# Second-order attention stage: units of one 128-token tile, or of two 64-token chunks from two batches

## Chip, core, metric

One Trainium2 chip, one of its cores. The metric is the device time of one execution in microseconds (us), lower is better. Before the change the kernel takes 3574.15 us, the median of three runs (3573.76 to 3574.67).

## What is computed

The reference is a chain of eight residual layers over x[8, 1024, 256] in float32. The change touches the fifth layer alone, a second-order linear attention with 16 heads of 32 columns and a decay of 0.99 per token:

```python
def step(carry, qkv):
    S_K, C_QV, G = carry
    q_t, k_t, v_t = qkv
    C_prev = GAMMA * C_QV
    k_C = jnp.einsum('bhk,bhkv->bhv', k_t, C_prev)
    G = GAMMA * G + k_t[..., :, None] * k_C[..., None, :]
    S_K = GAMMA * S_K + k_t[..., :, None] * k_t[..., None, :]
    C_QV = C_prev + q_t[..., :, None] * v_t[..., None, :]
    S_C = jnp.einsum('bhij,bhjv->bhiv', S_K, C_QV)
    o_t = jnp.einsum('bhk,bhkv->bhv', q_t, S_C - G)
    return ((S_K, C_QV, G), o_t)
...
x = x + _L1_attn_a_ref(_layernorm(x, axis=-1), L1_attn_a_Wq, L1_attn_a_Wk, L1_attn_a_Wv, L1_attn_a_Wo)
```

The other layers (local attention, two top-k expert layers, spectral attention, two tanh layers, window attention) are left as they are.

## The kernel before

The kernel runs its layers one after the other on one core; x stays in SBUF as 64 tiles of 128 tokens (`R.X`). `second_order_attention` (line 1544) is one stage. It does not walk token by token: it takes a tile of 128 tokens as a chunk, works out what the tokens of the chunk do to each other through masked 128x128 products, and carries a small state (three 32x32 matrices per head) from chunk to chunk.

**The unit.** One step `t` handles one tile for four heads (`HG = 4`, 4x32 = 128 partitions), so there are `NU` = 64 tiles x 4 head groups = 256 steps. Each engine has its own order of work, written out by hand as a loop over `t` (TensorE from line 1793, ScalarE 1908, VectorE 1988, GpSimd 2057), and semaphores tie them together. Within one step TensorE does, in this order:

- `keys_queries(t)` (L1647) and `queries_U(t-1)` (L1655): 8 and 4 matmuls on 32-row tiles of the array, 128 columns each, into the four banks `rows4`;
- `state_to_O(t-2)` (L1742, L1743): two matmuls over the whole array, against the state spread out to block-diagonal form by GpSimd (`spread_state`, L2045);
- `turn_KQ(t)`, `turn_W(t-1)` (L1668, L1669, L1662): three 128x128 transposes into `bankU`;
- a share of the projections of the tiles to come, in single-pass float32 (F32R), into `bankJ`: over 8 steps two of V (L1704), four of Q and K (L1684), the transposes of x (L1677), and two times the output projection `mix` (L1714), which goes to `bankX`;
- `state_to_UW(t)` (L1732, L1735): 8 matmuls on 32x32 tiles;
- `keys_to_U(t)`, `values_to_W(t)`, `values_to_O(t-1)` (L1749, L1756, L1763, L1766): 16 matmuls on 128x32 tiles; `state_products(t-1)` (L1777, L1780): 12 more with 32 columns.

ScalarE copies what comes out of PSUM (`copy_U` L1865, `copy_WT` L1869, `copy_O` L1878, `negate_W` L1892, `copy_KQ` L1898 and L1899, `copy_turned` L1852, `high_O` L1884); VectorE masks the 128x128 products (`mask_AB` L1965, `mask_P` L1973) and updates the state (`update` L1956); GpSimd applies the decay (L2032, L2039), spreads the state (L2045) and makes the low part of the output (`low_O` L2050).
## Time and profile before

| what | us |
|---|---|
| median of the runs | 3574.15 |
| profiled execution | 3566.9 |
| its span, first to last instruction | 3565.0 |
| this stage's loop, 1516 to 2750 us of the span | 1234 |
| TensorE busy in the loop | 1220.45 |
| ScalarE, VectorE, GpSimd busy in the loop | 577.49, 602.70, 518.98 |

The profile is of one execution. PE is TensorE's matmuls, PEld its weight loads, DVE VectorE, ACT ScalarE, POOL GpSimd. A matmul's end is modelled, so a PE that is busy all the time need not be full; the starts of instructions are the safer reading. PEclk is the share of TensorE's full clock that was granted. The queue named "instruction" carries the program itself to the engines.

### The profile page before, as it was taken

The numbers are of one execution on the slowest core, as the hardware profiler recorded it, in microseconds if no ns is written. First come the engines' busy times: TensorE is split into PE (matmuls) and PEld (weight loads), VectorE is DVE, ScalarE is ACT, GpSimd is POOL, SyncE is SP. The second block draws the span as 40 slices with busy tenths as digits, with TensorE's granted clock in tenths as the row PEclk, the third lists the DMA queues.
The fourth block names the chain that finished last, engine by engine and source line by source line (L and its number), as shares of the span: only waits on it lengthen the run. The fifth ranks groups of instructions, "written<-read, shape, count | busy, mean of one in ns | idle before, by whom it ended". The sixth has DMA issues, their size and how long they took to land. (4 is left out here: it accounts for less than half of the span.)

```text
span 3565.0 us, 133004 instructions
## 1 busy us (share of the span) xinstructions
PE 3316.4 (93%) x52918; PEld 2936.6 (82%) x52918; DVE 2212.0 (62%) x6377; ACT 2101.5 (59%) x6626; POOL 1505.2 (42%) x2318
## 2 busy tenths in 40 slices
PE   8939999799956999899999999999998999999998
PEld 8939999777746999888888888888887878888877
DVE  6675555678775555545544444444444788888887
ACT  5555655455445555444444444444443699999996
POOL 5754656300014665343434334344443633333225
PEclk9969999999977999999999999999999999999999
DMA  4143443512144443500000000000000143333333
GB/s 130 49 157 91 97 93 62 163 33 65 52 138 128 89 98 75 151 3 3 3 3 3 3 3 3 3 3 3 3 3 16 38 124 112 119 112 101 105 98 100
DMA packets 203003, 235.05 MB, mean 66 GB/s; under 512 B 18064, under 2 KB 183072, under 8 KB 202400
## 3 DMA queue, kind: packets, MB, share of 16 engines
q1 hardware_dynamic: 177824, 192.99, 17.1%
q0 software_dynamic: 24576, 33.57, 5.6%
q8 instruction: 433, 7.09, 0.8%
q14 instruction: 170, 1.39, 0.1%
HBM read 147.46 MB, written 79.04 MB: 64 GB/s over the span
## 5 line engine op out<-in xcount | busy, mean ns | idle before, releaser
L2513 ACT ACTIVATE wa_S<-wa_S,wa_top 128x192 f32<-128x192 f32 x1024 | 461.9, 472 | 38.7 <-DVE wa_top L2609 38.7
L1965 DVE TENSOR_TENSOR so_raw<-so_rows,so_masks 128x1024 f32<-128x1024 f32 x256 | 313.4, 1224 | 225.0 <-PE so_rows L1655 216.4
L2609 DVE CUSTOM_DVE_ANT_0 wa_S<-wa_bank,wa_band 128x192 f32<-128x192 f32 x1024 | 299.4, 348 | 3.6 <-issue 3.6
L2045 POOL TENSOR_TENSOR so_spread<-so_state,so_head 128x256 f32<-128x256 f32 x224 | 137.4, 613 | 336.5 <-PE so_bankC L1743 305.4
L1956 DVE SCALAR_TENSOR_TENSOR so_state<-so_state,so_bankX 128x96 f32<-128x96 f32 x192 | 48.8, 254 | 347.4 <-PE so_bankX L1780 347.4
L2050 POOL TENSOR_TENSOR so_OT<-so_O,so_OT 128x128 fp32r<-128x128 f32 x256 | 117.0, 457 | 343.3 <-ACT so_OT L1884 343.2
L1878 ACT COPY so_O<-so_bankC 128x128 f32<-128x128 f32 x256 | 68.1, 266 | 318.2 <-PE so_bankC L1743 318.1
L650 POOL DMA_INDIRECT sum_dram<-y,rows x128 | 223.8, 1749 | 29.5 <-issue 27.5
L2401 PE MATMUL wa_bank<-ident,wa_S 128*128 128x128 f32 x1536 | 220.9, 277 | 7.7 <-ACT wa_probT L2520 4.7
L2513 ACT ACTIVATION_READ_ACCUMULATOR wa_S<-wa_S,wa_top 128x1 f32 x1024 | 219.8, 215 | 0.0
L728 ACT ACTIVATE m4e_hT<-m_bank,m4e_bias 128x256 fp32r<-128x256 f32 x256 | 126.5, 494 | 150.1 <-PE m_bank L680 144.0
L728 ACT ACTIVATE m2e_hT<-m_bank,m2e_bias 128x256 fp32r<-128x256 f32 x256 | 125.9, 492 | 149.2 <-PE m_bank L680 142.8
L1684 PE MATMUL so_bankJ<-so_xnT,so_w 128*128 128x256 f32 x1500 | 207.8, 287 | 4.7 <-DVE so_xnT L1945 4.7
L2401 PEld LDWEIGHTS wa_bank<-ident,wa_S 128*128 128x128 f32 x1536 | 172.9, 140 | 36.1 <-ACT wa_S L2513 16.3
L680 PE MATMUL m_bank<-m4e_exT,m_w_parts 128*128 128x256 f32 x1536 | 189.9, 283 | 0.4 <-ACT m4e_h L728 0.4
L680 PE MATMUL m_bank<-m2e_exT,m_w_parts 128*128 128x256 f32 x1536 | 189.9, 283 | 0.0
L1684 PEld LDWEIGHTS so_bankJ<-so_xnT,so_w 128*128 128x128 f32 x1500 | 185.5, 190 | 5.1 <-DVE so_xnT L1945 5.1
L694 PE MATMUL m_bank<-m_w_parts,m4e_hT 128*128 128x256 f32 x1536 | 187.0, 281 | 0.6 <-DVE m4e_pre L775 0.6
L694 PE MATMUL m_bank<-m_w_parts,m2e_hT 128*128 128x256 f32 x1536 | 187.0, 281 | 0.6 <-DVE m2e_pre L775 0.6
L680 PEld LDWEIGHTS m_bank<-m4e_exT,m_w_parts 128*128 128x128 f32 x1536 | 184.2, 190 | 0.6 <-ACT m4e_h L728 0.6
L694 PEld LDWEIGHTS m_bank<-m_w_parts,m2e_hT 128*128 128x128 f32 x1536 | 184.0, 188 | 0.8 <-issue 0.8
L694 PEld LDWEIGHTS m_bank<-m_w_parts,m4e_hT 128*128 128x128 f32 x1536 | 184.0, 188 | 0.8 <-issue 0.8
(457 smaller groups left out, 9977.6 us busy)
## 6 DMA issues: line engine op xcount, KB each, us to landing
m_w_raw<-in_L_ffn_W_dram SPq DMA_DIRECT2D x64, 512.0 KB, 3.6
wa_V<-wa_V_dram SPq DMA_DIRECT2D x256, 128.0 KB, 2.6
sum_dram<-X SPq DMA_DIRECT2D x16, 1024.0 KB, 4.7
X<-sum_dram SPq DMA_DIRECT2D x16, 1024.0 KB, 8.2
wa_V_dram<-wa_V_new SPq DMA_DIRECT2D x32, 512.0 KB, 4.2
wa_V_rest<-wa_V_dram SPq DMA_DIRECT2D x128, 128.0 KB, 3.0
X<-in_L_attn_a_x_dram SPq DMA_DIRECT2D x8, 1024.0 KB, 10.9
xn_dram<-m2r_xn SPq DMA_DIRECT2D x16, 512.0 KB, 4.5
```

Source lines behind the costliest of these rows:

```text
L650: nc.gpsimd.indirect_dma_start(out=summed, out_offset=bass.IndirectOffsetOnAxis(ap=rows[:, s, u:u + 1], axis=0), in_=y[:, s % 2, u, :], in ...
L680: last = nc.tensor.matmul(bank[:, 0:2 * P], w_parts[:, par, a, c, f * P:(f + 1) * P], exT[:, s % 2, b, c], start=(n == 0), stop=(n == len( ...
L694: last = nc.tensor.matmul(by[u][:, 0:HID], hT[:, s % 2, a, f, u * P:(u + 1) * P], w_parts[:, par, b, 2 + f // QF, f % QF * HID:(f % QF + 1 ...
L728: last = nc.scalar.activation(to, bh[f % 4][:, 0:2 * P], ACT.Gelu_apprx_tanh, bias=bias[:, par, f:f + 1])
L1684: last = nc.tensor.matmul(bank[:, 2 * k * P:2 * (k + 1) * P], w[:, a, n, c, cols], xnT[:, b, c], start=(m == 0), stop=(m == 2 * len(PARTS) ...
L1878: nc.scalar.copy(O[:, t % UT], bC[:, P:2 * P]).then_inc(s_["O_copied"], 1)
L1965: nc.vector.tensor_tensor(AB[:, t % 2].rearrange("p h m t -> p h (m t)"), rows4[:, :, 0:2 * P], masks[:].rearrange("p m t -> p (m t)")[:, ...
L2045: nc.gpsimd.tensor_tensor(whole[:, t % UT], new[:, :, None, :].broadcast_to([P, 2, HG, DK]), head[:, None, :, None].broadcast_to([P, 2, HG ...
L2050: nc.gpsimd.tensor_tensor(OT[:, 1, t % (2 * UT)], O[:, t % UT], OT[:, 0, t % (2 * UT)].bitcast(F32), ALU.subtract).then_inc(s_["O_ready"], 1)
L2401: last = nc.tensor.transpose(to[:, h * P:(h + 1) * P], of, R.ident[:])
L2513: nc.scalar.activation(S[:, n % 2, z], S[:, n % 2, z], ACT.Exp, bias=top[:, n % 2, z:z + 1], scale=-1.0, accum_out=sums[:, i % 2, SET * c ...
L2609: nc.vector.tensor_tensor_reduce(out=S[:, n % 2, z], in0=bS[g][:, eo * SPAN:(eo + 1) * SPAN], in1=band[:], scale=-(D ** -0.5), scalar=3e38 ...
```

## The change

A unit becomes 64 tokens of two batches (`CHUNK` = 64, index `k`), still for four heads, so that the number of steps stays 256. Products that were 128x128 per head are now two of 64x64 (32x64 tiles), products over 128 tokens are two over 64 (64x32 tiles, one per batch, into two banks `cols`). The state's share of the output is computed on 32x32 tiles from the plain state, each head into the partitions of the next, and `spread_state` and its array go. `queries_U` and the outputs run a step later (`t-2`); VectorE copies the state's share out of `bankX` and adds it (`copy_from_state`, `add_O`) in place of ScalarE's `copy_O`; `copy_U` and `copy_WT` become one `copy_UW`; the three transposes share `bankX` and one semaphore; the output projection goes to `bankJ`, both tiles of a pair in the fourth step of eight, and the projections of Q and K to the last four. V and KW, KQe and AB get a third buffer. The order in which the 64 tiles of x are taken changes (pairs from two batches). GpSimd's `decayed`, `decayed_U`, `low_O` and `normalize` keep their sizes. The loads at the start: the output weights come in two DMAs, the masks at half size, `head` is gone.

The diff, cut; removed lines are left out where the kernel above has them:

```diff
+    CHUNK = P // 2
+    STEPS = SEQ // CHUNK
+        AB = raw[:, 0:3 * HG * P].rearrange("p (b h m t) -> p b h m t", b=3, h=HG, m=2)
+        PT = raw[:, 3 * HG * P:4 * HG * P].rearrange("p (b h t) -> p b h t", b=2, h=HG)
+        VRING = 3
+        V = sb("V", [P, VRING, UT, P])
+        KW, KQe = sb("KW", [P, 3, 2, P]), sb("KQe", [P, 3, 2, P])
+        UW, Ug = sb("UW", [P, 2, 2, P]), sb("Ug", [P, 2, P])
+        O, OT = sb("O", [P, UT, P]), sb("OT", [P, 2, UT, 2, 2, CHUNK], F32R)
+        from_state = sb("from_state", [P, 2, P])
+        rows4, cols = ps("rows", (P, HG, 512)), ps("cols", (P, 2, 512))
+        bX, bJ = (ps(f"bank{n}") for n in "XJ")
+        AT_U, AT_W, AT_O = (slice(n * CHUNK, (n + 1) * CHUNK) for n in range(3))
+        AT_S = slice(3 * CHUNK, 3 * CHUNK + 3 * DK)
...
+        def row_tile(p, half):
+            return (2 * (p // TB) + half) * TB + p % TB
+        def mixed_at(t):
+            return t // (2 * UT) - 1 if t % (2 * UT) == MIX_AT and t > MIX_AT else None
+                for to, name in ((masks[:, 0], "upper"), (masks[:, 1], "lower"), (decay_t[:], "decay_t"), (to_end[:], "to_end")):
+                out_rows = A["L1_attn_a_Wo"].rearrange("(u p) d -> p u d", p=P)
+                sp.dma_start(wo_raw[DK:P], out_rows[0:P - DK]).then_inc(s_["o_loaded"], 16)
+                sp.dma_start(wo_raw[0:DK], out_rows[P - DK:P]).then_inc(s_["o_loaded"], 16)
...
                 def keys_queries(t):
+                    ring, u, j = place(t)
+                    pe.wait_ge(s_["QT_ready"], halves_to(chunk(t)))
+                    pe.wait_ge(s_["KT_ready"], halves_to(chunk(t)))
                     for m, (a, b) in enumerate(((KT, QT), (QT, KT))):
                         for h in range(HG):
...
+                            for k in range(2):
+                                last = nc.tensor.matmul(rows4[half_rows(k), h, m * CHUNK:(m + 1) * CHUNK],
+                                                        a[head_rows(h), ring, u, j, half_rows(k)], b[head_rows(h), ring, u, j, half_rows(k)],
+                                                        start=True, stop=True, tile_position=(h * DK, k * CHUNK))
...
                 def queries_U(t):
+                    ring, u, j = place(t)
+                    pe.wait_ge(s_["UW_ready"], t + 1)
                     for h in range(HG):
...
+                        for k in range(2):
+                            last = nc.tensor.matmul(rows4[half_rows(k), h, 2 * CHUNK:3 * CHUNK],
+                                                    QT[head_rows(h), ring, u, j, half_rows(k)], UW[head_rows(h), t % 2, 0, half_rows(k)],
+                                                    start=True, stop=True, tile_position=(h * DK, k * CHUNK))
...
+                def turn(t):
+                    if t >= 3:
+                        pe.wait_ge(s_["from_state_ready"], carries_to(t - 3))
+                    if t < NU:
+                        at = place(t)
+                        nc.tensor.transpose(bX[:, P:2 * P], KT[(slice(None), *at)], R.ident[:])
+                        last = nc.tensor.transpose(bX[:, 2 * P:3 * P], QT[(slice(None), *at)], R.ident[:])
                     if t >= 1:
...
+                        pe.wait_ge(s_["UW_ready"], t)
...
+                            pe.wait_ge(s_["x_ready"], 2 * (p - 1))
                     elif job <= 2:
                         pe.wait_ge(s_["QT_ready"], 2 * p + job)
...
+                def mix(p):
+                    pe.wait_ge(s_["O_ready"], 2 * UT * (p + 1))
+                    if p + 1 < NT // 2:
+                        pe.wait_ge(s_["V_ready"], 2 * (p + 2))
+                    if p + 2 < NT // 2:
+                        pe.wait_ge(s_["xT_ready"], p + 3)
+                    for half in range(2):
+                        for m, (a, b, u) in enumerate((a, b, u) for a, b in PARTS for u in range(UT)):
+                            last = nc.tensor.matmul(bJ[:, half * HID:(half + 1) * HID], OT[:, a, u, half].rearrange("p j t -> p (j t)"), wo[:, b, u],
+                                                    start=(m == 0), stop=(m == UT * len(PARTS) - 1))
...
+                def state_of(t, k, m, h):
+                    return state[head_rows(h), chunk(t) % 2, t % UT, k, m]
+                def decayed_of(of, t, h, k):
+                    return of[head_rows(h), chunk(t) % 2, t % UT, half_rows(k)]
+                def states_to_UW(t, n):
+                    m, k = divmod(n, 2)
                     for h in range(HG):
...
+                        if m == 0:
+                            nc.tensor.matmul(cols[head_rows(h), k, AT_U], state_of(t, k, 0, h), decayed_of(QTg, t, h, k),
+                                             start=True, stop=False, tile_position=(h * DK, h * DK))
+                        else:
+                            nc.tensor.matmul(cols[head_rows(h), k, AT_W], state_of(t, k, 2, h), decayed_of(KTg, t, h, k),
+                                             start=False, stop=False, tile_position=(h * DK, h * DK), skip_group_check=True)
+                def states_to_O(t, n):
+                    k, m = divmod(n, 2)
                     for h in range(HG):
...
+                        of = Ug[head_rows(h), t % 2, half_rows(k)] if m == 0 else decayed_of(QTg, t, h, k)
+                        nc.tensor.matmul(bX[turned_rows(h), half_rows(k)], state_of(t, k, 2 - m, h), of, start=(m == 0), stop=(m == 1),
+                                         tile_position=(h * DK, (h + 1) % HG * DK))
                 def keys_to_U(t):
+                    for k in range(2):
+                        for h in range(HG):
+                            nc.tensor.matmul(cols[head_rows(h), k, AT_U], KW[half_rows(k), t % 3, 0, head_rows(h)], AB[half_rows(k), t % 3, h, 0],
+                                             start=not carries(t), stop=True, tile_position=(k * CHUNK, h * DK))
                 def values_to_W(t):
+                    for k in range(2):
+                        for h in range(HG):
+                            last = nc.tensor.matmul(cols[head_rows(h), k, AT_W], V[half_rows(k), chunk(t) % VRING, t % UT, head_rows(h)],
+                                                    AB[half_rows(k), t % 3, h, 1], start=not carries(t), stop=True,
+                                                    tile_position=(k * CHUNK, h * DK), skip_group_check=True)
...
+                        for h in range(HG):
+                            nc.tensor.matmul(cols[turned_rows(h), k, AT_O], V[half_rows(k), chunk(t) % VRING, t % UT, head_rows(h)],
+                                             PT[half_rows(k), t % 2, h], start=True, stop=False, tile_position=(k * CHUNK, (h + 1) % HG * DK))
+                    for k in range(2):
+                        for h in range(HG):
+                            last = nc.tensor.matmul(cols[turned_rows(h), k, AT_O], KW[half_rows(k), t % 3, 1, head_rows(h)],
+                                                    AB[half_rows(k), t % 3, h, 0], start=False, stop=True,
...
+                for t in range(NU + 4):
+                    if 1 <= t <= NU:
+                        pe.wait_ge(s_["AB_ready"], t)
+                    if 3 <= t < NU + 3:
+                        pe.wait_ge(s_["PT_ready"], t - 2)
                     if t < NU:
                         last = keys_queries(t)
...
+                    if 2 <= t < NU + 2:
+                        last = queries_U(t - 2)
+                    if t < NU + 2:
+                        last.then_inc(s_["row_done"], 1)
                     if t <= NU:
...
+                        turn(t)
+                    in_pair, p = t % (2 * UT), t // (2 * UT)
+                    if in_pair < 2 and p < NT // 2:
                         project_V(2 * p + in_pair)
...
+                    if in_pair == TURN_AT and p + 1 < NT // 2:
                         turn_x(p + 1)
...
+                    if mixed_at(t) is not None:
+                        mix(mixed_at(t))
+                    if in_pair >= PROJECT_AT and p + 1 < NT // 2:
+                        project_next(in_pair - PROJECT_AT, p + 1)
+                    if t >= NU + 2:
+                        continue
                     if t < NU:
                         pe.wait_ge(s_["K_ready"], t + 1)
                         pe.wait_ge(s_["KQe_ready"], t + 1)
...
+                    if t >= 1:
+                        pe.wait_ge(s_["UW_ready"], min(t, NU))
+                        pe.wait_ge(s_["W_ready"], min(t, NU))
+                    if t >= 3:
+                        pe.wait_ge(s_["O_added"], t - 2)
+                        pe.wait_ge(s_["S_ready"], updates_to(t - 3))
+                    to_UW, to_O = t < NU and carries(t), t >= 2 and carries(t - 2)
+                    if to_UW:
+                        pe.wait_ge(s_["QTg_ready"], carrying_chunks_to(chunk(t)))
+                        pe.wait_ge(s_["KTg_ready"], carrying_chunks_to(chunk(t)))
+                    if to_O:
+                        pe.wait_ge(s_["Ug_ready"], carries_to(t - 2))
+                    for n in range(4):
+                        if to_UW:
+                            states_to_UW(t, n)
+                        if to_O:
+                            states_to_O(t - 2, n)
                     if t < NU:
                         keys_to_U(t)
                         last = values_to_W(t)
...
+                    if t >= 2:
+                        last = values_to_O(t - 2)
+                        if updates(t - 2):
+                            last = state_products(t - 2)
+                    last.then_inc(s_["C_done"], 1)
...
+                def copy_UW(t):
+                    act.wait_ge(s_["C_done"], t + 1)
+                    if t >= 2:
+                        act.wait_ge(s_["row_done"], t + 1)
+                        act.wait_ge(s_["turned"], t)
                         act.wait_ge(s_["Ug_ready"], carries_to(t - 2))
+                    nc.scalar.copy(UW[:, t % 2].rearrange("p m (k s) -> p k m s", k=2),
+                                   cols[:, :, 0:2 * CHUNK].rearrange("p k (m s) -> p k m s", m=2)).then_inc(s_["UW_ready"], 1)
                 def copy_KQ(t):
+                    if t >= 3:
+                        act.wait_ge(s_["C_done"], t)
+                def negate_W(t):
+                    act.wait_ge(s_["turned"], t + 2)
+                    nc.scalar.mul(KW[:, t % 3, 1], bX[:, 3 * P:4 * P], -1.0).then_inc(s_["W_ready"], 1)
...
+                def copy_from_state(t):
+                    dve.wait_ge(s_["C_done"], t + 3)
+                    if t >= 2:
+                        dve.wait_ge(s_["O_added"], t - 1)
+                    nc.vector.tensor_copy(from_state[:, t % 2], bX[:, 0:P]).then_inc(s_["from_state_ready"], 1)
+                def add_O(t):
+                    dve.wait_ge(s_["C_done"], t + 3)
+                    dve.wait_ge(s_["UW_ready"], min(t + 3, NU))
+                    if t >= UT:
+                        dve.wait_ge(s_["O_ready"], t - UT + 1)
+                    to = O[:, t % UT].rearrange("p (k s) -> p k s", k=2)
+                    if carries(t):
+                        dve.wait_ge(s_["from_state_ready"], carries_to(t))
+                        ins = nc.vector.tensor_tensor(to, cols[:, :, AT_O], from_state[:, t % 2].rearrange("p (k s) -> p k s", k=2), ALU.add)
+                    else:
+                        ins = nc.vector.tensor_copy(to, cols[:, :, AT_O])
+                    ins.then_inc(s_["O_added"], 1)
...
+                    dve.wait_ge(s_["C_done"], t + 3)
```

`values_to_O` and `state_products` change in the same way: 16 matmuls of 64 columns on 64x32 tiles in place of 8 of 128, and 8 of 64 columns with 8 of 32 in place of 12 of 32. VectorE's masks work on 128x512 and 128x256 elements in place of 128x1024 and 128x512, its update on 128x192 in place of 128x96.

## Rows read from the trace of the kernel before

**Rows 1.** Head of the page: span, then busy us of each engine, share, instructions
```profile
span 3565.0 us, 133004 instructions
PE 3316.4 (93%) x52918; PEld 2936.6 (82%) x52918; DVE 2212.0 (62%) x6377; ACT 2101.5 (59%) x6626; POOL 1505.2 (42%) x2318
```

**Rows 2.** The page's 40 slices of the span, 89 us each
```profile
PE   8939999799956999899999999999998999999998
...
PEclk9969999999977999999999999999999999999999
```

**Rows 3.** The stage's loop by engine: us, busy and instructions, PEclk, DMA share, GB/s
```profile
1516.00:2750.00 1234.00, 1220.45 (x27688) 1058.03 (x27684) 602.70 (x935) 577.49 (x2010) 518.98 (x874) 1.00 0.01 3
```

**Rows 4.** Timeline of PE in one unit: start, us, line, count
```profile
2087.86 0.50 PE L1647 MATMUL so_rows<-so_QT,so_KT 32*128 32x128 f32 x8
...
2088.41 0.40 PE L1655 MATMUL so_rows<-so_U,so_QT 32*128 32x128 f32 x8
2088.74 0.49 PE L1742 MATMUL so_bankC<-so_Ug,so_spread 128*128 128x128 f32 x2
...
2089.29 0.27 PE L1668 MATMUL so_bankU<-ident,so_KT 128*128 128x128 f32 x1
...
2091.13 0.31 PE L1732 MATMUL so_bankU<-so_QTg,so_state 32*32 32x128 f32 x4
...
2091.51 0.43 PE L1749 MATMUL so_bankU<-so_raw,so_KW 128*32 128x128 f32 x8
2091.75 0.40 PE L1756 MATMUL so_bankC<-so_raw,so_V 128*32 128x128 f32 x8
...
2092.40 0.31 PE L1777 MATMUL so_bankX<-so_KW,so_KQe 128*32 128x32 f32 x16
2092.53 0.25 PE L1780 MATMUL so_bankX<-so_V,so_KQe 128*32 128x32 f32 x8
2092.70 0.39 PE L1647 MATMUL so_rows<-so_QT,so_KT 32*128 32x128 f32 x4
```

**Rows 5.** Groups by line of 2000 to 2600 us: count, busy, mean ns
```profile
L1965 DVE TENSOR_TENSOR so_raw<-so_rows,so_masks 128x1024 f32<-128x1024 f32 x125 | 153.0, 1224 | 106.7 <-PE so_rows L1655 106.7
L1973 DVE TENSOR_TENSOR so_raw<-so_rows,so_masks 128x512 f32<-128x512 f32 x124 | 84.3, 680 | 0.0
L2045 POOL TENSOR_TENSOR so_spread<-so_state,so_head 128x256 f32<-128x256 f32 x109 | 66.9, 613 | 157.4 <-PE so_bankC L1743 150.4 <-DVE so_state L1958 7.0
L1869 ACT COPY so_WT<-so_bankC 128x128 f32<-128x128 f32 x124 | 32.9, 265 | 49.5 <-PE so_bankC L1766 49.0
L1956 DVE SCALAR_TENSOR_TENSOR so_state<-so_state,so_bankX 128x96 f32<-128x96 f32 x96 | 24.4, 254 | 177.8 <-PE so_bankX L1780 177.8
```

**Rows 6.** Timeline of ACT behind one set of transposes; in brackets the idle time before
```profile
2301.86 0.28 ACT L1892 ACTIVATE so_KW<-so_bankU 128x128 f32<-128x128 f32 x1 [1.08 <-PE so_bankU L1662]
...
2302.18 0.49 ACT L1899 ACTIVATE so_KQe<-so_bankU,so_to_end 128x256 f32<-128x256 f32 x1
```

**Rows 7.** The instruction queue's packets, MB, share: whole page, then the stage's loop
```profile
q8 instruction: 433, 7.09, 0.8%
...
q8 instruction: 224, 3.67, 1.3%
```

**Rows 8.** Timeline of PE's weight loads around two stops
```profile
2217.75 0.30 PEld L1655 LDWEIGHTS so_rows<-so_U,so_QT 32*128 32x128 f32 x6 [0.58 <-issue]
...
2223.93 0.29 PEld L1655 LDWEIGHTS so_rows<-so_U,so_QT 32*128 32x128 f32 x2 [0.60 <-issue]
```

**Rows 9.** Windows: what ran between the two stops
```profile
2217.75:2223.92 6.17, 5.77 (x123) 5.08 (x123) 3.09 (x5) 2.28 (x8) 2.75 (x4) 1.00 0.01 3
```

**Rows 10.** DMA in 40 slots of 0.225 us, window 2215 to 2224: instruction packets alone
```profile
DMA  0020000000000000000000000000300000000000
```

**Rows 11.** DMA in 40 slots of 0.25 us, window 1991 to 2001: instruction packets alone
```profile
DMA  0003000000000000000400000000000000000300
```

More of the change, by code:

```diff
@@ L1782, in state_products @@
-                    last.then_inc(s_["S_done"], 1)
+                    first, last = AT_S.start, AT_S.stop
+                    for k in range(2):
+                        for h in range(HG):
+                            nc.tensor.matmul(cols[head_rows(h), k, first:first + 2 * DK].rearrange("p (m v) -> p m v", m=2),
+                                             KQe[half_rows(k), t % 3, 0, head_rows(h)], KW[half_rows(k), t % 3, :, head_rows(h)],
+                                             start=True, stop=True, tile_position=(k * CHUNK, h * DK))
@@ L1784, in _ @@
+                    for k in range(2):
+                        for h in range(HG):
+                            done = nc.tensor.matmul(cols[head_rows(h), k, last - DK:last], KQe[half_rows(k), t % 3, 1, head_rows(h)],
+                                                    V[half_rows(k), chunk(t) % VRING, t % UT, head_rows(h)],
+                                                    start=True, stop=True, tile_position=(k * CHUNK, h * DK))
+                    return done
                 for _ in range(30):
-                    nc.tensor.matmul(bC[:, 0:P], R.ident[:], R.ident[:], start=True, stop=True)
+                    nc.tensor.matmul(cols[:, 0, 0:P], R.ident[:], R.ident[:], start=True, stop=True)
@@ L1982, in stats @@
+                def stats(p, half):
+                    dve.wait_ge(s_["x_ready"], 2 * p + half + 1)
+                    i = row_tile(p, half)
                     nc.vector.bn_stats(R.raw[:, i, :], R.X[:, i, :])
                 low_xT(0)
-                dve.wait_ge(s_["loaded"], 5 * 16)
+                dve.wait_ge(s_["loaded"], 4 * 16)
                 dve.wait_ge(s_["w_high"], 4)
                 nc.vector.tensor_tensor(wo[:, 1], wo_raw, wo[:, 0].bitcast(F32), ALU.subtract).then_inc(s_["w_ready"], 1)
-                for t in range(NU + 4):
-                    if 2 <= t < NU + 2 and updates(t - 2):
-                        update(t - 2)
+                for t in range(NU + 5):
+                    if 3 <= t < NU + 3 and carries(t - 3):
+                        copy_from_state(t - 3)
+                    if 3 <= t < NU + 3:
+                        add_O(t - 3)
@@ L1991, in _ @@
                     if t < NU:
                         mask_AB(t)
+                    if 2 <= t < NU + 2:
+                        mask_P(t - 2)
+                    if 3 <= t < NU + 3 and updates(t - 3):
+                        update(t - 3)
                     if STATS_AT <= t < STATS_AT + NT // 2:
@@ L2071, in _ @@
                         decayed(KTg, KT, "KT_ready", "KTg_ready", i + 1)
[L2072 to L2073 removed]
+                    if t >= 3:
+                        low_O(t - 3)
 def window_attention(nc, R, A, C):
```

368 lines of the change are left out of this document (107 added, 261 removed).

## The prediction, made before the changed kernel had run

> **What bounds the kernel now.** I read the page's totals first, then its slices, then one window for the stage that the change touches, then the timeline of TensorE in one unit, and at last the queue that carries the program. TensorE is busy for 3316.4 of 3565.0 us [rows 1], and the slices show it at eight or nine tenths nearly everywhere; slices 18 to 30, one kind of stretch with an even clock, are the stage [rows 2]. Its loop is 1234.00 us long with TensorE busy for 1220.45, VectorE for 602.70, ScalarE for 577.49 and GpSimd for 518.98 [rows 3]. So the stage is TensorE's, at 1234 / 256 = 4.82 us a unit: one period from the first L1647 to the next is 4.84 us [rows 4].
>
> Inside the unit the starts tell what a set of matmuls costs. The four sets from L1749 to L1777 take 2092.40 - 2091.51 = 0.89 us, 0.22 each; a set is 8 recorded MATMULs of 128 columns, four tiles side by side, so a round of four is 0.11 [rows 4]. The 16 with 32 columns of L1777 take 0.13, or 0.03 a round [rows 4]. Array time goes by columns, and tiles that don't share rows and columns run together.
>
> The other limit doesn't show in the busy time. The program comes to TensorE in packets of 16 KB, 224 in the loop [rows 7] for 27688 + 27684 recorded matmuls and weight loads [rows 3]: one packet for 247 of them, and 1234 / 224 = 5.5 us for each. Twice within this window TensorE stops in the middle of a set that waits for nothing, 0.58 us at 2217.75 and 0.60 us at 2223.93, "issue" in both [rows 8]. Between the two it ran 123 matmuls and 123 loads, 246 [rows 9]: exactly one packet's worth. And only two packets arrive, in slot 2 (2215.5) and in slot 28 (2221.3) [rows 10], each 2.3 to 2.6 us ahead of the restart. I read this so: TensorE used up a block, stood until the next was there, and the one after was asked for only when it had begun this one. Nothing was kept in store beyond one block.
>
> **The change, part by part.**
>
> *Instructions.* A float32 matmul is four instructions of the stream (8 MATMULs and 8 loads for four calls). Before, a unit that carries state has 8 + 4 + 2 + 8 + 16 + 12 = 50 such matmuls and 3 transposes of two: 206. After: 16 for the rows, 8 for `queries_U`, 16 `states_to_UW`, 16 `states_to_O`, 8 `keys_to_U`, 8 `values_to_W`, 16 `values_to_O`, 16 `state_products`: 104 matmuls, 422 instructions. Projections, `mix` and the transposes of x stay at 5,632 for the stage. Over 256 units, 16 of them without a state to carry and 16 without one to update (3,072 fewer), that is 108,032 - 3,072 + 5,632 = 110,592, against 55,372. At 247 a packet: 448 packets in place of 224.
>
> *Array time.* Gone are, a unit, 3 row sets (0.66), the two whole-array products (0.43), `state_to_UW` (0.26), four sets (0.89) and the 32-column ones (0.2): about 2.4 us [rows 4]. In their place stand 208 MATMULs, nearly all of 64 columns, eight tiles side by side: 26 rounds at half of 0.11, about 1.5 us. An estimate; that eight tiles run side by side is supported by L1732 and L1735, 16 MATMULs of 128 columns between 2091.13 and 2091.51, 0.024 us each where four abreast would cost 0.028 [rows 4]. If the supply keeps up, this frees 0.92 us a unit, 235 us in all.
>
> *VectorE.* `mask_AB` goes from 1224 ns to the 680 of 128x512, `mask_P` from 680 to some 400 (between 254 for 96 columns and 680 for 512), `update` from 254 to some 340 by the same line, and the two new operations on 128x128 are some 270 each, as ScalarE's 265 [rows 5]. 2.16 us becomes 1.96 us. Under a unit of at least 3.9 us this costs nothing.
>
> *ScalarE and GpSimd.* Three copies of 265 ns become one of 256 columns at the 490 of L1899 [rows 6], and 613 ns of GpSimd go with L2045 [rows 5]. Neither is late now. Cost nil.
>
> *New waits.* `turn` waits for `from_state_ready`, the share of the V projection for `x_ready`, `mix` for `V_ready` and `xT_ready`; behind each stand the whole of TensorE's queue and so the other engines a step later. The awaited work is one step old or more in each case. Two come nearer than that: `copy_UW` needs the end of the last set and then 0.49 us plus the hand-over, and `turn(t+1)` waits for it behind the rows and `queries_U`, which are 3 rounds times 0.06 plus a little, some 0.45 us; 0.1 to 0.2 us a unit may be open. The chain that makes KW and KQe takes ScalarE from 2301.86 to 2302.18 + 0.49 = 2302.67, 0.81 us [rows 6], and with the hand-over ahead of it, which I put at 0.4, it ends 1.2 us behind the transposes; projections cover it in seven steps of eight, and in the eighth, with only the transposes of x (0.44 us), some 0.8 us are open: 32 x 0.8 = 25 us. Together 50 us if TensorE is otherwise free, between 0 and 100; nothing if it stands for instructions anyway, since the others catch up meanwhile.
>
> *Start loads.* As many DMAs on SP's queue as before, smaller, ahead of the loop in the shadow of the layer before: nil, from -1 to +2 us.
>
> *The supply.* A unit's work on the array after the change would be 3.9 us for 110,592 / 256 = 432 instructions, so a packet every 2.2 us; the trace has none that close. The nearest rows: three in 1991 to 2001 stand 4.0 and 4.5 us apart, the shortest spacing that I found in the loop, with TensorE not standing [rows 11]; and the starved one is 2223.93 - 2217.75 = 6.18 us [rows 8]. The time from a packet's start to the restart is 2.3 to 2.6 us [rows 8, 10]; the time from the first instruction of a block to the next packet's start is, counted on by 247 from these stops, 0.6 to 1.2 us in most blocks and 3 to 4 in about one in five (the ones where TensorE came to a long wait just then; 2217.75 to 2221.3 is one [rows 8, 10]). So 3.2 us in four blocks of five and 6.2 in one: 3.8 us a packet. Taken: 448 x 3.8 = 1702 us for the loop, against 1234: +468. Bounds: 3.0 (0.6 + 2.4, no block late) gives 1344, +110; 5.0 (three in five late) gives 2240, +1006.
>
> The sum, made against the profiled execution: 3566.9 + 468 = 4035; the median of the runs stands 7 us over it, so 4042, rounded to 4040.
>
> **The rivals.**
>
> *The array decides and the supply hides* (12 in 100). Stops are few in the loop now, and their length is small. Then 3566.9 - 235 + 50 + 7 = 3389, between 3330 and 3450. Against it: the stop at 2223.93 is one whole block after another, with a packet landed 2.4 us before [rows 8, 10]. The Trainium skill ("Runtime: NRT & Kernel Launch", Instruction fetch mechanics) speaks for it: a block boundary costs one DMA request that is "mostly hidden", as the sequencer dispatches more slowly than the refill. By that rule the change would gain; the trace, with 0.58 and 0.60 us of stop one block apart, doesn't agree with it at this pace.
>
> *The supply decides but at 2.75 us a packet* (3 in 100): 448 x 2.75 = 1232, no change, 3573. It needs a request sooner than any block in the trace shows.
>
> *The supply is always late* (5 in 100): every block like the starved one, 448 x 6.2 = 2778, +1544, 5118. It needs each block to meet a long wait just behind its start; possible if every unit has one at the same place, and the clock might fall as well: at the seams between stages, where TensorE idles, slices show 7 tenths [rows 2].
>
> *The change doesn't double the stream* (in the first rival's chance): were a 64-column matmul issued as fewer instructions, packets would stay under 448; the counts by line will tell.
>
> The rival on the other side is the first: from 2.75 us a packet downwards the kernel gets faster, and it decides once supply and array meet at 1234 us.
>
> **How the numbers follow.** Forecast (supply binds between 3.0 and 5.0 us a packet) 80, the array 12, no change 3, always late 5. The forecast's own ends are 3684 and 4580. The range from 3650 to 4600 leaves out the other three, 2 in 10 together. Faster by over 0.2%, about what a measurement of this kernel can tell from no change, is 0.12; within it 0.03; slower 0.85.
>
> **What would show it.** In the profile after: 440 to 460 packets of the instruction queue in the loop; TensorE idle by "issue" in the middle of sets, at places that move along by 247 instructions, 1 us or more each; packet starts evenly 3 to 4 us apart; PE busy far under 98% of the loop; the waits of TensorE for the other engines short. If the loop is about 1000 to 1100 us and the idle time names VectorE or ScalarE, the array's rival was right. If PEclk in the loop falls under 1.00, a part of the time is the clock's and the price of a packet is that much less. If masks or updates cost other than 680 and 340 ns, the part on VectorE is wrong, but not the sum. The prediction is wrong if packets come closer than 2.75 us apart while TensorE runs.

## The result and the profile after

The changed kernel takes 4165.68 us (median; 4161.28 to 4168.1), against 3574.41 for the one before: a ratio of 1.1656, 95% interval 1.1641 to 1.167. The forecast was 4040 in a range of 3650 to 4600. The profiled execution took 4166.8 us with a span of 4165.0.

The head of the page of the changed kernel, its slices for TensorE and the granted clock (104 us each), and the instruction queue:

```profile
span 4165.0 us, 187534 instructions
...
PE 3491.9 (84%) x80438; PEld 3084.9 (74%) x80438; DVE 2152.0 (52%) x6889; ACT 2008.1 (48%) x6114; POOL 1391.3 (33%) x2118
...
PE   9949997998599977777777777777777789999998
...
PEclk9969999999699998888888889888888789999999
...
q8 instruction: 646, 10.58, 1.1%
```

[rows 2] had the stage at nine tenths; it is at seven now and longer. The same loop in one window (columns as in [rows 3]), and its packets of the instruction queue, read up to 3345 us:

```profile
1518.00:3344.00 1826.00, 1389.06 (x55140) 1199.48 (x55140) 539.47 (x1440) 482.55 (x1499) 403.57 (x673) 0.86 0.02 4
...
q8 instruction: 437, 7.16, 1.6%
```

The loop went from 1234 to 1826 us, +592, and all the rest of the program from 2333 to 2341. The matmuls and loads doubled, 55,372 to 110,280; the packets went from 224 [rows 7] to 437, and TensorE stands for 437 us of the loop, where it stood for 14 before. The waits of TensorE in the loop by line: in all, how often, the longest:

```profile
PE so_rows L1658 <- issue: 101.0, 60, 2.3
PE so_rows L1668 <- issue: 56.0, 33, 2.3
PE so_cols L1798 <- issue: 51.7, 29, 2.5
PE so_cols L1793 <- issue: 49.8, 28, 2.4
PE so_cols L1780 <- issue: 38.8, 23, 2.5
PE so_cols L1771 <- issue: 37.3, 25, 2.4
PE so_cols L1784 <- issue: 34.6, 25, 2.1
PE so_cols L1747 <- DVE so_state L1983: 9.2, 9, 1.3
PE so_cols L1747 <- POOL so_QTg L2066: 8.2, 9, 1.0
PE so_cols L1747 <- ACT so_KW L1916: 5.5, 10, 1.2
```

Seven sets of matmuls, for which the profile names nothing that they wait for, stand for 369 us in 223 stops, up to 2.5 us long. Before, TensorE stood for 14 us in the whole loop, and the stops of [rows 8] are 0.6 us. The waits for other engines, which the new order might have brought, are 23 us in these three rows. The other engines' operations (columns as in [rows 5]):

```profile
L1992 DVE TENSOR_TENSOR so_raw<-so_rows,so_masks 128x512 f32<-128x512 f32 x256 | 176.8, 691 | 197.7 <-PE so_rows L1668 186.9 <-PE so_rows L1658 9.7 <-issue 0.2
L2000 DVE TENSOR_TENSOR so_raw<-so_rows,so_masks 128x256 f32<-128x256 f32 x255 | 105.9, 415 | 0.0
...
L1896 ACT COPY so_UW<-so_cols 128x256 f32<-128x256 f32 x256 | 95.3, 372 | 612.9 <-PE so_cols L1798 589.1 <-PE so_cols L1784 23.3 <-PE so_cols L1771 0.5
...
L1983 DVE SCALAR_TENSOR_TENSOR so_state<-so_state,so_cols 128x192 f32<-128x192 f32 x224 | 77.2, 345 | 0.0
...
L1972 DVE TENSOR_TENSOR so_O<-so_cols,so_from_state 128x128 f32<-128x128 f32 x239 | 69.8, 292 | 41.0 <-ACT so_UW L1896 40.6 <-POOL so_OT L2078 0.2
```

Where they stand idle it is for TensorE, except for 41 us of the output's sum (L1972), which waits for ScalarE's `copy_UW`, and that one waits for TensorE. One place, closer: the timeline of PE around a stop, and the DMA slots of 2130 to 2139 (0.225 us each, as in [rows 10]):

```profile
2132.36 0.52 PE L1658 MATMUL so_rows<-so_KT,so_QT 32*64 32x64 f32 x16 [1.96 <-issue]
2132.63 0.46 PE L1668 MATMUL so_rows<-so_UW,so_QT 32*64 32x64 f32 x16
2133.02 0.47 PE L1678 MATMUL so_bankX<-ident,so_KT 128*128 128x128 f32 x1
...
2133.57 2.91 PE L1721 MATMUL so_bankJ<-so_w,so_xnT 128*128 128x512 f32 x6
2136.41 0.33 PE L1747 MATMUL so_cols<-so_QTg,so_state 32*32 32x64 f32 x4
...
DMA  2000000000000000000000000020000000000000
```

A packet lands from 2130.0 on, TensorE restarts 2.3 us behind its start, and the next packet starts in slot 26 (2135.9), 3.5 us behind the restart. Such late ones are a minority. Over the loop, packets stand 3.3 us apart at the closest, 3.9 in the median, and over 5.5 in one of eight (53 of 436); the mean is 1826 / 437 = 4.18.

### The profile page after: what moved, and what is told of

The parts are those of the page before. It is cut to its first block and busy times, and to the rows that moved or that the text cites. A ratio compares the mean times of both kernels' runs of the same rounds, so it can differ in the third digit from the quotient of the medians.

```text
span 4165.0 us, 187534 instructions
## 1 busy us (share of the span) xinstructions
PE 3491.9 (84%) x80438; PEld 3084.9 (74%) x80438; DVE 2152.0 (52%) x6889; ACT 2008.1 (48%) x6114; POOL 1391.3 (33%) x2118
## 5 line engine op out<-in xcount | busy, mean ns | idle before, releaser
L1962 DVE COPY so_from_state<-so_bankX 128x128 f32<-128x128 f32 x240 | 70.0, 292 | 890.7 <-PE so_cols L1798 833.7
L1896 ACT COPY so_UW<-so_cols 128x256 f32<-128x256 f32 x256 | 95.3, 372 | 612.9 <-PE so_cols L1798 589.1
L2073 POOL TENSOR_TENSOR so_Ug<-so_UW,so_decay_t 128x128 f32<-128x128 f32 x240 | 109.1, 454 | 551.8 <-ACT so_UW L1896 551.8
L1992 DVE TENSOR_TENSOR so_raw<-so_rows,so_masks 128x512 f32<-128x512 f32 x256 | 176.8, 691 | 197.7 <-PE so_rows L1668 186.9
L1910 ACT COPY so_KW<-so_bankX 128x128 f32<-128x128 f32 x256 | 68.2, 266 | 435.4 <-PE so_bankX L1682 434.3
L1699 PE MATMUL so_bankJ<-so_xnT,so_w 128*128 128x256 f32 x1500 | 255.1, 329 | 11.3 <-DVE so_xnT L1956 6.0
L1699 PEld LDWEIGHTS so_bankJ<-so_xnT,so_w 128*128 128x128 f32 x1500 | 229.2, 230 | 14.9 <-issue 8.6
L1668 PE MATMUL so_rows<-so_UW,so_QT 32*64 32x64 f32 x4096 | 140.1, 259 | 56.0 <-issue 56.0
L680 PEld LDWEIGHTS m_bank<-m2e_exT,m_w_parts 128*128 128x128 f32 x1536 | 185.4, 191 | 0.0
```

Source lines behind the costliest of these rows:

```text
L680: last = nc.tensor.matmul(bank[:, 0:2 * P], w_parts[:, par, a, c, f * P:(f + 1) * P], exT[:, s % 2, b, c], start=(n == 0), stop=(n == len( ...
L1668: last = nc.tensor.matmul(rows4[half_rows(k), h, 2 * CHUNK:3 * CHUNK], QT[head_rows(h), ring, u, j, half_rows(k)], UW[head_rows(h), t % 2, ...
L1699: last = nc.tensor.matmul(bank[:, 2 * k * P:2 * (k + 1) * P], w[:, a, n, c, at], xnT[:, b, c], start=(m == 0), stop=(m == 2 * len(PARTS) - 1))
L1992: nc.vector.tensor_tensor(AB[:, t % 3].rearrange("p h m t -> p h (m t)"), rows4[:, :, 0:2 * CHUNK], masks[:].rearrange("p m t -> p (m t)") ...
L2073: nc.gpsimd.tensor_tensor(Ug[:, t % 2], UW[:, t % 2, 0], decay_t[:], ALU.mult).then_inc(s_["Ug_ready"], 1)
```

## The experiments

Two theories stood against each other, with a third beside them. *Supply*: TensorE waits for its own program, one packet at a time. *Array*: the small matmuls take the time, or a clock lowered by idleness does. *Order*: the new waits do. First, the stream alone was made longer, with the order of before.

```diff
+                PAD = 14
...
+                    for n in range(PAD * HG):
+                        h = n % HG
+                        nc.tensor.matmul(bU[head_rows(h), 0:8], state_of(t, 0, h), QTg[head_rows(h), tile(t) % 2, t % UT, 0:8],
+                                         start=True, stop=True, tile_position=(h * DK, h * DK))
```

> The kernel before, with 56 extra matmuls of 8 columns on 32x32 tiles ahead of the state's share in each of the 224 units that carry state; their result is overwritten, nothing else changes. They are 224 instructions a unit, 50,176 in all, 196 packets of 256: 224 + 196 = 420. Theory (the supply of instructions sets the pace, 4.18 us a packet as in the changed kernel's loop of 1826 us and 437 packets): the loop takes 420 x 4.18 = 1756 us, +522, total 4096; TensorE stops by issue in the middle of sets. Rival (the array or the issue of a matmul sets it, 0.0088 us for a MATMUL with its load as in the densest sets): 112 x 0.0088 x 224 = +221, total 3795. Rival (new waits of the changed order were the cause): the order is that of before, so no more than the +221.

Measured: 4315.51 us, ratio 1.2096 (1.2065 to 1.2127). The loop and its packets:

```profile
1517.00:3487.00 1970.00, 1635.14 (x52775) 1425.15 (x52775) 602.18 (x933) 582.33 (x2007) 526.70 (x874) 0.92 0.01 4
...
q8 instruction: 420, 6.88, 1.4%
```

The packets came out as counted, but at 4.69 us each and not 4.18, so the loop is 214 us longer than the theory's 1756; what makes the packets dearer here comes further down. The order of the changed kernel is not needed for its slowness. The array's part can't explain it: a pair of load and matmul costs 0.0093 us at the full clock and 0.0148 at the lower (both in the bursts below), so 233 to 371 us of the 736 are for the 112 pairs in 224 units; the rest, 365 us at least, is the supply's. The same edit with `PAD = 4`:

> The kernel before with 16 extra matmuls of 8 columns a unit (64 instructions, 14,336 in all, 56 packets, 280 in the loop), overwritten by what follows. Their own time, 0.0148 us a MATMUL as in the burst, is 32 x 0.0148 x 224 = +106 us, which makes 1340 us and 4.8 us a packet, above the 3.7 of a packet that isn't late. Theory (only late packets, 5.6 to 6.3 us, can starve TensorE at this pace): +106 to +170, total 3680 to 3745. Rival (each packet costs 4.2 to 4.7 us whatever the pace): 280 x 4.2 = 1176, no cost from the supply, so +106 at most. Rival (price as in the run with 224 more instructions a unit, 4.69 us, added for each packet): 56 x 4.69 = +263.

Measured: 3741.73 us, 1.048 (1.0457 to 1.0503); the loop 1402 us with 280 packets. That is +168, at the upper end of the first theory. Both rivals miss it: no more than +106, and +263. The expectation had taken the pair at 0.0148 us; the clock in this loop is 1.00, so its 32 pairs in 224 units are 67 us, and 101 are left for a stream that already fails now and then at 5.0 us a packet. Then the changed kernel with fewer instructions, its order kept.

```diff
-                        if updates(t - 2):
+                        if updates(t - 2) and t < 8:
                             last = state_products(t - 2)
```

> The changed kernel without the products that feed the state (state_products, 16 matmuls, 64 instructions a unit) from step 8 on; the update then reads old values. 232 units less 64 instructions: 14,848, 58 packets of 437. Theory (supply): 379 x 4.18 = 1584 us for the loop, -242, total 3924. Rival (array): 32 MATMULs less a unit at 0.0088 to 0.0125 us: -65 to -93 us, total 4070 to 4100. Rival (waits between engines): no wait is removed, so -0 to -20.

Measured: 3959.63 us, 1.109 (1.1066 to 1.1113); the loop 1617 us with 378 packets, -209 for 59 packets. Between the theory's -242 and the array's -93, nearer to the first. With two more sets left out as well:

```diff
-                        last = queries_U(t - 2)
+                        last = queries_U(t - 2) if t < 8 or t >= NU else last
...
-                    for k in range(2):
+                    for k in range(2 if t < 8 else 0):
```

> The changed kernel from step 8 on without three of its sets: the products that feed the state (64 instructions a unit), the product of queries and U (32), the second half of the values' output (32). 437 - 116 = 321 packets. Theory (supply, price falling nowhere): 321 x 4.2 = 1348 us for the loop, total 3690, three points with 437 and 378 packets on one line through the origin. Rival (below some count the array and the engines' turns set the pace): the array's work is then near 3.6 us a unit, 920 us in all, so a loop above 1348 would have to come from waits, named in the trace; a loop well under 1348 would mean that the price of a packet falls with the array's work.

Measured: 3736.98 us, 1.0463 (1.0446 to 1.0481); the loop 1393 us with 316 packets. The three points, 437, 378 and 316 packets, have 4.18, 4.28 and 4.41 us a packet: nearly one line, with a little that doesn't go with the packets. TensorE stands for 254 us of this loop, 206 of them by issue and 34 for other engines, and even with 30% of the small matmuls gone the stage is slower than before, with all of its 128x128 work.

The other side, array work with hardly any instructions, in the changed kernel and in the one before:

```diff
+                        for _ in range(4):
+                            nc.tensor.matmul(bank[:, 2 * k * P:2 * (k + 1) * P], w[:, 0, n, 0, at], xnT[:, 0, 0], start=True, stop=True)
...
+                    for _ in range(4):
+                        nc.tensor.matmul(bJ[:], xnT[:, 0, 0, i % 2 * P:(i % 2 + 1) * P], w[:, 0, 2, 0], start=True, stop=True)
```

> The changed kernel with four extra F32R matmuls ahead of each projection of 256 or 512 columns, overwritten by it: 0.9 us of array work in six steps of eight, 0.68 us a unit and 173 us in all, for 10 instructions a unit, 10 packets. Theory (supply): +42 us at most from 10 packets, the rest of the array work goes into stops that are there anyway; the granted clock, 0.86 in the loop, rises as the array is busier. Rival (array, or a clock lowered by idleness that itself costs the time): +173 in the first case, and in the second the clock back at 1.0 gives back up to 14 percent of the busy 1387 us, -190 + 173.

> The kernel before with the same four extra F32R matmuls ahead of each projection as were put into the changed kernel, where they cost 38 us. Theory (before is bound by the array, the changed kernel by the supply): here they cost their array time, 0.9 us in six steps of eight, 173 us in all (150 to 180), total 3743. Rival (before has slack, or is bound by supply as well): 40 us or less.

Measured: 4204.07 us in the changed kernel (1.1775, 1.175 to 1.1799; loop 1861, 447 packets) and 3739.69 in the one before (1.0468, 1.045 to 1.0485; loop 1399). The windows of the two loops:

```profile
1524.00:3385.00 1861.00, 1502.76 (x56404) 1323.05 (x56404) 538.81 (x1441) 481.60 (x1499) 403.64 (x673) 0.89 0.02 4
```

```profile
1521.00:2920.00 1399.00, 1390.35 (x28935) 1219.26 (x28935) 601.85 (x933) 578.39 (x2008) 520.64 (x874) 1.00 0.01 3
```

The same work costs 165 us of the loop where the array binds and 35 where the supply does, and 35 is about what ten packets cost. It is the clearest of the pairs: array time is all but free in the changed stage.

Next, the price of a packet by itself: one burst of 8,192 instructions that wait for nothing, in the kernel before.

```diff
+                def burst(t):
+                    for n in range(2048):
+                        h = n % HG
+                        nc.tensor.matmul(bU[head_rows(h), 0:8], state_of(t, 0, h), QTg[head_rows(h), tile(t) % 2, t % UT, 0:8],
+                                         start=True, stop=True, tile_position=(h * DK, h * DK))
...
+                    if t == 101:
+                        burst(t)
```

> The kernel before, with one burst of 2048 matmuls of 8 columns (8192 instructions, 32 packets) in one unit, nothing waited for within it. It shows what a packet costs when TensorE waits for nothing else. Theory (one packet in store, the next asked for when TensorE enters a block): 32 stops, one each 256 instructions, packets 3.3 to 3.8 us apart, none of the 5.6 us that the changed kernel shows for one in eight, since these come from waits just behind a block's start; +106 to +122 us. Rival (the queue delivers as fast as asked, the price lies in the instructions): 4096 MATMULs at 0.0088 us are 36 us, +36. Rival (late packets come by chance, not from waits): intervals of over 5 us in about one of eight here too.

Measured: 3686.14 us against 3570.15, +116. The bursts ran once each; what counts is their traces. The timeline of PE:

```profile
2006.75 1.89 PE L1730 MATMUL so_bankU<-so_QTg,so_state 32*32 32x8 f32 x128 [2.02 <-issue]
2010.50 1.89 PE L1730 MATMUL so_bankU<-so_QTg,so_state 32*32 32x8 f32 x128 [1.86 <-issue]
2014.52 1.89 PE L1730 MATMUL so_bankU<-so_QTg,so_state 32*32 32x8 f32 x128 [2.14 <-issue]
...
2029.80 1.89 PE L1730 MATMUL so_bankU<-so_QTg,so_state 32*32 32x8 f32 x128 [1.59 <-issue]
2033.28 1.89 PE L1730 MATMUL so_bankU<-so_QTg,so_state 32*32 32x8 f32 x128 [1.59 <-issue]
```

It shows the mechanism bare: 128 matmuls with their 128 loads, then a stop, thirty times over. From 2006.75 to 2118.32 they are 30 blocks, 3.72 us each, of which the block itself needs 1.9. The steps are 3.47, 3.75 or 4.02 us, never 5. The granted clock in this stretch is 0.50, and that isn't what sets the pace: in the burst with long matmuls (below) a stretch at 1.00 has its packets just as far apart. Windows of the two, the first of this burst, the second of that one:

```profile
2006.00:2118.00 112.00, 56.62 (x3840) 53.90 (x3840) 0.00 (x0) 0.00 (x0) 0.00 (x0) 0.50 0.02 4
```

```profile
2033.00:2056.00 23.00, 17.59 (x791) 16.05 (x790) 0.00 (x0) 0.00 (x0) 0.00 (x0) 1.00 0.02 4
```

The first holds 7,680 instructions in 112 us, the second 1,581 in 23: 3.73 and 3.72 us for 256. The Trainium skill ("Runtime: NRT & Kernel Launch", Instruction fetch mechanics) has refills in blocks of 256 instructions, which the 128 + 128 show, and a cost that is "mostly hidden", which holds at 5.5 us a packet and not at these rates.

So 3.72 is the floor and 4.18 the changed kernel's mean; some three quarters of the difference is late packets: 74 of the 436 intervals are over 5.0 us, 5.73 in the mean, and the others have 3.86. Where do they come from? Of some 340 blocks whose start can be read from a stop in the changed kernel, the next packet starts 1.1 to 1.7 us behind the block's first instruction in most, and 2.8 to 3.8 us behind it in 56. Of these 56, 54 belong to blocks that start in the row sets (L1658, L1668), that is, ahead of the projections and the waits for K, Q and W. No block that starts in the sets from L1747 to L1798 has one. In the run with 14 extra matmuls per head it is the same stretch (L1647, L1655, the state's share of the output), and nearly a third of the blocks: hence 4.69. Four bursts asked which part of that stretch does it. The long matmuls alone (a group of 56 small matmuls and 12 F32R ones), and a wait alone:

> The kernel before with a burst in one unit of 40 groups, each of 56 matmuls of 8 columns (224 instructions) and 12 F32R matmuls of 256 columns (24 instructions, 1.6 us of array), with no wait. 9,920 instructions, 39 packets. Theory of waits: no late packet, 3.5 to 4.0 us apart all through, +145 us in all. Rival (long matmuls): the packets whose block starts within 1 to 1.5 us ahead of the 12 long ones are late, 5 to 6 us apart, a quarter to a third of them: +165 us or more.

> The kernel before with a burst in one unit of 40 groups, each of 61 matmuls of 8 columns (244 instructions) and then a wait for ScalarE, which answers with four copies of 128 columns, about 1.2 to 1.8 us. A group is a little shorter than a packet of 256, so the block's start moves through the group by about 12 instructions each time. Theory (a packet is late when TensorE's instruction stream stands at a wait soon behind the block's start, as it seems from the places of late packets in the changed kernel): packets 3.7 us apart while the wait is far behind the block's start, and 5 to 6 us apart in the quarter to third of the groups where it comes within 1 to 1.5 us of it. Rival (long matmuls ahead of the stream, not waits, make it late): none over 4.3 us beyond what the wait itself adds in a line.

Measured: 3711.52 and 3717.06 us (3571.32 before beside them). In both, packets come 3.3 to 4.4 us apart through the whole burst; neither the long matmuls nor a wait of 1.0 us makes a late one. Then both together, and a longer wait:

> The kernel before with a burst in one unit of 40 groups: 52 matmuls of 8 columns and one more that tells ScalarE (212 instructions), 12 F32R matmuls of 256 columns (24 instructions, 1.6 us), and then a wait for ScalarE's answer, four copies of 512 columns, some 2.4 us. So TensorE's sequencer comes to the wait while the long matmuls ahead of it still run, as it does at the wait for K and KQe behind the projections in the real unit. 236 instructions a group, the block's start moves by 20 each time. Theory A (a packet is late when the sequencer stands at a wait for about 2 us or more soon behind the block's start; neither the 1.0 us wait alone nor the 1.6 us of long matmuls alone did it): in about a quarter to a third of the groups the next packet starts 3 us or more behind the block's first instruction, against 1.15 in the others, and packets are 5 to 6 us apart there. Theory B (lateness has another cause in the unit): 3.5 to 4.3 us all through, except what the group's own length gives.

> As the burst with a wait of 1.0 us, 40 groups of 244 instructions with no long matmuls, but ScalarE answers with five copies of 512 columns, about 2.9 us. Theory A (a long stand of the sequencer alone makes a packet late): with the wait soon behind the block's start, the next packet starts about 1.1 us behind the end of the wait, 3 to 4 us behind the block's first instruction. Theory C (it takes long matmuls in the queue ahead of the wait): the packet starts 1.1 to 1.5 us behind the block's first instruction in every group, while TensorE waits.

Measured: 3707.94 and 3763.15 us (3570.36 before). Each has two late packets in 40 groups, not a quarter of them: in the first, one 5.4 and one 5.6 us behind its forerunner; in the second 7.4 and 8.3. The one of the burst with waits of 2.8 us, as PE's timeline and the DMA slots of 2020 to 2030 (0.25 us) show it:

```profile
2022.66 1.78 PE L1732 MATMUL so_bankU<-so_QTg,so_state 32*32 32x8 f32 x120 [2.79 <-ACT so_scratch L1941]
...
2027.31 1.78 PE L1732 MATMUL so_bankU<-so_QTg,so_state 32*32 32x8 f32 x120 [2.79 <-ACT so_scratch L1941]
...
DMA  0002000000000000000000000000000003000000
```

The packet in slot 33 (2028.3) starts 1.0 us behind the end of the wait at 2027.31. So a long wait can hold a packet back until it ends, but in these bursts only where the block's start falls on one narrow place ahead of it: the two late ones of the second burst are 98 us apart, 21 groups, which is about once round for a start that moves by 12 of 244 instructions a group. Both theories of these runs, as put, are wrong in the share.

In the real unit the place is wide, and the trace of the changed kernel shows where it lies. Take the 93 blocks that start in the row sets, and count the matmuls and loads from there to the row of waits ahead of L1747 (L1837 to L1850). Where they are 84 or fewer, 54 blocks of 57 have a late packet, and the three others have the output projection in between; where they are 85 or more, none of 36 has. In all 54 the packet starts 0.6 to 1.6 us behind the last of these waits, 1.0 in the median, as in the burst. The lower clock isn't the cause: 47 of 78 are late at the full clock, and 7 of 15 at the lower. So the late packets are those of blocks that start close ahead of these waits. Why the stretch is 84 instructions long here and so short in the bursts isn't settled. The real unit has several waits one behind the other; that wasn't tried.

The last run asked for a version better than both: fewer instructions and less array work in the kernel before, by taking K, Q and U in rounded form so that the row products need one pass.

```diff
-        QT, KT = sb("QT", [P, 2, UT, 2, P]), sb("KT", [P, 2, UT, 2, P])
+        QT, KT = sb("QT", [P, 2, UT, 2, P], F32R), sb("KT", [P, 2, UT, 2, P], F32R)
...
-        U, Ug = sb("U", [P, 2, P]), sb("Ug", [P, 2, P])
+        U, Ug = sb("U", [P, 2, P], F32R), sb("Ug", [P, 2, P])
```

> The kernel before with K, Q and U for the row products (keys_queries, queries_U) kept in the rounded float32 format, so that these 12 matmuls of a unit are one pass instead of two: 24 instructions a unit fewer, 24 packets of 224, and half the array work of the three row sets. Theory (before is bound by the array, so half of 0.66 us a unit is won, and nothing by the packets): -84 us, total 3487. Rival (a one-pass matmul of 128 columns takes as long as two passes): within 10 us. Rival (before is bound by its packets): 24 x 5.5 = -132.

Measured: 3460.03 us, 0.9691 (0.9675 to 0.9707), the best of all. A unit in PE's timeline, and the loop:

```profile
2089.56 0.33 PE L1647 MATMUL so_rows<-so_QT,so_KT 32*128 32x128 f32 x4
2089.72 0.28 PE L1647 MATMUL so_rows<-so_KT,so_QT 32*128 32x128 f32 x4
2089.83 0.28 PE L1655 MATMUL so_rows<-so_U,so_QT 32*128 32x128 f32 x4
2090.04 0.33 PE L1668 MATMUL so_bankU<-ident,so_KT 128*128 128x128 f32 x1
...
1516.00:2639.00 1123.00, 1114.46 (x24615) 967.43 (x24615) 601.71 (x934) 576.87 (x2007) 519.34 (x874) 1.00 0.01 3
```

The row sets take 2090.04 - 2089.56 = 0.48 us where [rows 4] had 2088.74 - 2087.86 = 0.88: 0.40 less in 256 units is 102 of the 110 us gained. It is won on the array, as the packets, at 5.6 us each, don't bind. The expectation's -84 was short because it took the row sets as 0.66 us; the total alone would stand between it and the -132 of the packets, and it is the timeline that tells them apart.

## Why the prediction was right, point by point

- *What bounds the kernel.* Right: TensorE's array before, with the supply close behind. Extra array work costs its full time there.
- *The count.* 448 packets were forecast, 437 came. The divisor was the 247 matmuls and loads of the old loop, which leaves out the waits that are instructions of their own. The traces record 2,036 of these in the old loop and 1,610 in the new one; with them a packet holds 256 instructions in both, as in the burst. The new order has fewer waits to a packet, and so 252 matmuls and loads.
- *The price.* 3.8 us forecast, 4.18 measured, and this is the term that was mis-sized. Its first part, 3.2 for a packet that isn't late, measured 3.72 in the burst: from a packet's start to the restart it is 2.3 to 2.7 us as read, but the next starts 1.1 to 1.7 us behind the block's first instruction, not 0.6 to 1.2. The late ones, forecast at 6.2 us in one block of five, are 56 of some 340, one in six, and stand some 5.7 us apart. That they come from waits close behind the block's start was read rightly. The errors of count and price go against each other: 448 x 3.8 = 1702, 437 x 4.18 = 1826.
- *Array time.* 235 us were to be freed if the supply kept up. It can't be read off, since it didn't. `keys_to_U` takes 0.14 us to the next set (2503.44 to 2503.58), where 0.22 stood before and 0.11 was forecast, but the two state sets with their 64 MATMULs took 0.78 us (2502.66 to 2503.44), 0.012 each and not the 0.007 of eight tiles side by side. The work of before was mis-read too. By the starts in [rows 4] the row sets take 0.88 us and not 0.66, the whole-array products 0.55 and not 0.43, the state's two sets 0.38 and not 0.26, the 32-column ones 0.30 and not 0.2: 3.0 us with the four sets, not 2.4. In the changed kernel the row sets take 0.71 (2504.80 to 2505.51), the state's 0.78, and the sets from L1764 on 1.08 in units without a stop there: 2.6 us. So an estimate of what a full supply would free is 0.4 us a unit, some 110 us and not 235, and the rival "array" was too hopeful by that.
- *Other engines.* 691, 415 and 345 ns for masks and update (680, 400 and 340 forecast), 292 for the two new operations (270), 372 for `copy_UW` (490). All hidden.
- *New waits.* Nothing if TensorE stands for instructions, up to 100 us otherwise; 23 us are named for other engines.
- *The rivals.* "Supply hides" and "2.75 us a packet" fell with the first run. "Always late" fell with the share of late packets. The clock's part of it was real but small in effect: 0.86 in the loop instead of 1.00, while the bursts have the same pace at 0.50 and at 1.00, and the changed kernel with more array work, at 0.89, isn't faster.

## What to carry to other kernels

Count TensorE's instructions, not only its columns: a float32 matmul is four, and a stream that uses up 256 of them in less than some 5 us starts to stop, and under 3.7 us it must. Splitting a product into smaller tiles cuts its array time (0.22 to 0.14 us for the set of `keys_to_U`, not the half) and doubles its stream, so it pays only while the time per packet stays above that. The supply doesn't show in busy shares; it shows as idle time by "issue" in sets that wait for nothing, and in the spacing of the instruction queue's packets.

## What the runs showed of the hardware beyond the forecast

- A packet's cycle without any wait is 3.47, 3.75 or 4.02 us, in steps of about 0.27, and 3.72 in the mean.
- A load and matmul pair of 8 columns on four tiles in turn costs 0.0093 us at the full clock (1.04 us for 112, from 2012.25 to 2013.30 in the burst with long matmuls) and 0.0148 at the lower (1.89 / 128).
- The supply's pace doesn't hang on TensorE's clock: 3.73 us a packet at 0.50, 3.72 at 1.00.
- The lower clock comes with TensorE's idleness: 1.00 in the loop that stood for 14 us, 0.86 in the one that stood for 437. 6 F32R matmuls of 512 columns took 2.91 us at 2133.57, 1.2 us behind a stop of 1.96, against 1.64 at 1519.07. The granted clock was 0.50 in the one and 1.00 in the other, 1.2 and 2.4 GHz.
- A wait can hold back the next packet of program, which then starts 1.0 us behind its end: in the burst with waits of 2.8 us, and in the median of the 54 late blocks of the changed kernel.
- With the waits counted, a packet is 256 instructions of TensorE's stream in both loops: 57,408 in 224 packets before, 111,890 in 436 after.
